# Chunk attention: the scores for the row maxima over 64 rows of the array, even and odd chunk in its two halves, issued two pairs after four exponent tiles

## Time and profile before

| | us |
|---|---|
| median of three runs | 3944.57 (3942.08 to 3945.07) |
| profiled execution, its own time | 3944.43 |
| profiled execution, span of the trace | 3942.7 |
| PE / DVE / ACT / POOL busy over the span | 3455.3 / 2757.4 / 2286.2 / 2169.0 |
| steady part of the chunk attention, 188 to 691 us: PE / DVE / ACT busy | 501.02 / 432.56 / 360.41 of 503.00 |

### The profile page before, as it was taken

The page is one execution under the profiler, slowest core; times in us unless marked ns, Lnnn a source line. Parts: engine busy times, 40 slices in busy tenths (PEclk is TensorE's granted clock), DMA queues, the critical chain, the costliest instruction groups (busy, mean ns, idle before and its releaser), DMA issues. The chain is left out here.

```text
span 3942.7 us, 89530 instructions
## 1 busy us (share of the span) xinstructions
PE 3455.3 (88%) x30494; PEld 2111.7 (54%) x30494; DVE 2757.4 (70%) x7236; ACT 2286.2 (58%) x5520; POOL 2169.0 (55%) x2263
## 2 busy tenths in 40 slices
PE   5999999985695999999999999995958885987678
PEld 1333333325592566566566566563946774775456
DVE  6888888856454778878888888873437884655565
ACT  2777777763243666666666666662436671864367
POOL 3333333315544777888887888874422332754275
PEclk7999999995697999999999999997979997987879
DMA  5434334413452222222222222222633332110001
GB/s 100 61 59 60 60 60 62 62 17 101 137 193 67 48 55 50 51 56 55 53 57 51 51 57 51 50 55 75 199 92 81 89 82 43 44 45 5 0 1 44
DMA packets 414451, 254.32 MB, mean 65 GB/s; under 512 B 251418, under 2 KB 340434, under 8 KB 412722
## 3 DMA queue, kind: packets, MB, share of 16 engines
q1 hardware_dynamic: 403316, 226.43, 25.0%
q0 software_dynamic: 10688, 22.17, 1.8%
HBM read 91.61 MB, written 45.94 MB: 35 GB/s over the span
## 5 line engine op out<-in xcount | busy, mean ns | idle before, releaser
L2799 POOL TENSOR_TENSOR ra_prob<-ra_prob,ra_inverse 128x256 f32<-128x256 f32 (+3 forms) x512 | 631.1, 1255 | 250.5 <-DVE ra_inverse L3098 249.3
L2577 DVE TENSOR_REDUCE ca_mx<-ca_ps_s 128x2 f32<-128x1024 f32 x512 | 600.6, 1211 | 120.4 <-PE ca_ps_s L2449 120.2
L3012 ACT ACTIVATE ra_prob<-ra_ps_s,ra_low 128x128 f32<-128x128 f32 (+3 forms) x1024 | 533.6, 532 | 228.5 <-DVE ra_low L3078 225.8
L2514 ACT ACTIVATE ca_pT<-ca_ps_p 128x512 f32<-128x512 f32 x1024 | 544.9, 600 | 204.6 <-PE ca_ps_p L2459 203.1
L3078 DVE CUSTOM_DVE_ANT_0 ra_ps_s<-ra_ps_s,ra_mask 128x128 f32<-128x128 f32 (+3 forms) x1024 | 479.9, 510 | 44.1 <-PE ra_ps_s L2954 43.8
L2449 PE MATMUL ca_ps_s<-ca_kst,ca_qst 128*128 128x512 bf16 x1024 | 393.0, 389 | 24.4 <-DMA ca_kst<-ca_bounce 10.9
L2459 PE MATMUL ca_ps_p<-ca_qst,ca_kst 128*128 128x512 bf16 x1024 | 386.7, 383 | 5.5 <-ACT ca_pT L2514 4.2
L3018 ACT COPY ra_probT<-ra_ps_t 128x512 f32<-128x512 f32 x384 | 227.2, 592 | 254.2 <-PE ra_ps_t L2866 254.2
L2866 PE MATMUL ra_ps_t<-ident,ra_prob 128*128 128x128 f32 x2560 | 350.1, 276 | 3.3 <-ACT ra_probT L3018 2.1
L2954 PE MATMUL ra_ps_s<-ra_kz,ra_qz 64*128 64x128 f32 (+3 forms) x2048 | 348.1, 458 | 3.8 <-DMA ra_kz<-ra_rot 2.9
L2792 POOL TENSOR_TENSOR ra_rot<-ra_prod 128x512 f32<-128x512 f32 x256 | 320.6, 1273 | 40.6 <-DVE ra_prod L3087 40.6
(11 more groups left out here) (491 smaller groups left out, 7278.5 us busy)
## 6 DMA issues: line engine op xcount, KB each, us to landing
ra_qz<-ra_rot SPq DMA_DIRECT2D x512, 64.0 KB, 2.0
ra_kz<-ra_rot SPq DMA_DIRECT2D x512, 64.0 KB, 2.0
moe_w_own<-moe_w1T SPq DMA_DIRECT2D x71, 256.0 KB
moe_w_own<-router_w SPq DMA_DIRECT2D x71, 256.0 KB
ca_kst<-ca_bounce SPq DMA_DIRECT2D x256, 64.0 KB
ca_bounce<-ca_thirds SPq DMA_DIRECT2D x192, 64.0 KB
ca_qst<-ca_bounce SPq DMA_DIRECT2D x64, 192.0 KB
moe_hs<-moe_rows SPq DMA_DIRECT2D x71, 66.0 KB, 2.1
```

Source lines behind the costliest of these rows:

```text
L2514: nc.scalar.activation(pT[:, (NS * hp + u) % PRING, :], ps_p[n % NP][:], ACT.Exp).then_inc(sg["drained"], 1)
L2577: nc.vector.tensor_reduce(mx[:, hm % 2, 2 * j:2 * j + 2], ps_s[m % 2][:].rearrange("p (b k) -> p b k", b=2), AX.X, ALU.max)\
L2799: nc.gpsimd.tensor_tensor(at, at, inverse[:, n % PROB, 2 * tile:2 * tile + 2].unsqueeze(2).broadcast_to([P, 2, keys]), ALU.mult)\
L3012: nc.scalar.activation(prob[:, n % PROB, tile, head, 0:keys], part(n, tile)[:, head, :], ACT.Exp, bias=low[:, n % PROB, at:at + 1], scale= ...
```

```diff
-                        sp.dma_start(qst[ROWS:ROWS + 2, s, :], zeros).then_inc(qk_ready[s], 16)
                         for lo, hi in Q_ROWS:
                             sp.dma_start(qst[lo:hi, s, :]...)
                         for r, (_, tk) in enumerate(THIRDS):
                             sp.dma_start(kst[r * DK:(r + 1) * DK, s, :]...)
+                        wait(sp, sg["s_in"], PAIRS * (hf - 1))
+                        odd = bounce[s].rearrange("o (a two) x d g t -> two o (x d) a (g t)", two=2)[1]
+                        for lo, hi in Q_ROWS:
+                            sp.dma_start(qodd[ROWS + lo:ROWS + hi, hf % 2, :]..., odd[0, 0:hi - lo]).then_inc(odd_ready[hf % 2], 16)
+                        for r, (_, tk) in enumerate(THIRDS):
+                            sp.dma_start(kodd[ROWS + r * DK:ROWS + (r + 1) * DK, hf % 2, :]..., odd[1, tk * DK:(tk + 1) * DK])\
+                                .then_inc(odd_ready[hf % 2], 16)
...
-                def score(k, h):
-                    a, qt = k // 4, k % 4
-                    if k == 0:
+                def scores(j, h):
+                    a, qt = j // 4, j % 4
+                    if j == 0:
                         pe.wait_ge(qk_ready[h % RING], times(h, RING, COPIES))
-                    m = s_use[h, k // 2]
-                    out = pair(m) if k % 2 == 0 else ps_s[m % 2]
-                    ins = nc.tensor.matmul(out[:, k % 2 * 512:(k % 2 + 1) * 512], chunk(qst, P, h, a, qt), chunk(kst, P, h, a), start=True, stop=True)
-                    if k % 2:
-                        ins.then_inc(sg["s_in"], 1)
+                        pe.wait_ge(odd_ready[h % 2], times(h, 2, COPIES))
+                    out = pair(s_use[h, j])
+                    nc.tensor.matmul(out[:, 0:512], chunk(qst, ROWS, h, 2 * a, qt), chunk(kst, ROWS, h, 2 * a), start=True, stop=True)
+                    nc.tensor.matmul(out[:, 512:1024], qodd[ROWS:2 * ROWS, h % 2, a * 512 + qt * P:a * 512 + (qt + 1) * P],
+                                     kodd[ROWS:2 * ROWS, h % 2, a * 512:(a + 1) * 512], start=True, stop=True).then_inc(sg["s_in"], 1)
...
-                        if hm is not None:
-                            score(u, hm)
+                        if hm is not None and u % 4 == 3:
+                            for j in (u // 2 - 1, u // 2):
+                                scores(j, hm)
```

More of the change, by code:

```diff
@@ L2233, in chunk_attention @@
     Q_ROWS = ((0, 24), (24, 48), (48, 64))
-    COPIES = len(Q_ROWS) + len(THIRDS) + 1
+    COPIES = len(Q_ROWS) + len(THIRDS)
     RING = 4
-    VRING = 6
+    VRING, VW = 6, 16
     PRING = 12
@@ L2257, in chunk_attention @@
     sbounce = nc.dram_tensor(f"{name}_sbounce", (2, 2, NS, P), BF16, kind="Internal").ap()
-    zeros = nc.dram_tensor(f"{name}_zeros", (2, CG * HT), BF16, kind="Internal").ap()
     with ExitStack() as ctx:
@@ L2272, in chunk_attention @@
         kst = sb("kst", [P, RING, CG * HT], BF16)
-        vst = sb("vst", [P, VRING, NC, 4, 32])
+        qodd, kodd = sb("qodd", [P, 2, CG * HT // 2], BF16), sb("kodd", [P, 2, CG * HT // 2], BF16)
+        vst = sb("vst", [P, VRING, NC * 4 + 1, VW])
         mx = sb("mx", [P, 2, NS])
@@ L2284, in chunk_attention @@
         ps_p = [pb(f"ps_p{i}") for i in range(NP)]
-        loaded, prep, zeroed = sem("loaded"), sem("prep"), sem("zeroed")
+        loaded, prep = sem("loaded"), sem("prep")
         q_set, k_set, v_set = sem("q_set"), sem("k_set"), sem("v_set")
@@ L2294, in chunk_attention @@
         qk_ready = [sem(f"qk_ready{i}") for i in range(RING)]
+        odd_ready = [sem(f"odd_ready{i}") for i in range(2)]
         sbounced = [sem(f"sbounced{i}") for i in range(2)]
@@ L2307, in _ @@
                 sp.wait_ge(q_set, 1)
-                sp.dma_start(zeros, qst[ROWS:ROWS + 2, 0, :]).then_inc(zeroed, 16)
-                sp.wait_ge(zeroed, 16)
                 sp.wait_ge(k_set, 1)
@@ L2323, in body @@
                             sp.dma_start(kst[r * DK:(r + 1) * DK, s, :].rearrange("p (a c) -> p a c", a=NC), rows[1, tk * DK:(tk + 1) * DK]).then_inc(qk_ready[s], 16)
+                        wait(sp, sg["s_in"], PAIRS * (hf - 1))
+                        odd = bounce[s].rearrange("o (a two) x d g t -> two o (x d) a (g t)", two=2)[1]
+                        for lo, hi in Q_ROWS:
+                            sp.dma_start(qodd[ROWS + lo:ROWS + hi, hf % 2, :].rearrange("p (a c) -> p a c", a=NC // 2), odd[0, 0:hi - lo]).then_inc(odd_ready[hf % 2], 16)
+                        for r, (_, tk) in enumerate(THIRDS):
+                            sp.dma_start(kodd[ROWS + r * DK:ROWS + (r + 1) * DK, hf % 2, :].rearrange("p (a c) -> p a c", a=NC // 2), odd[1, tk * DK:(tk + 1) * DK])\
+                                .then_inc(odd_ready[hf % 2], 16)
                     if ht is not None:
@@ L2468, in values @@
                         a = 4 * g + b
-                        last = nc.tensor.matmul(ps_o[b * 32:(b + 1) * 32, :], vst[:, h % VRING, a, kt, :], pT[:, (NS * h + 4 * r + b) % PRING, :],
+                        last = nc.tensor.matmul(ps_o[b * 32:(b + 1) * 32, :], vst[:, h % VRING].rearrange("p n d -> p (n d)")[:, (4 * a + kt) * VW:(4 * a + kt) * VW + 32], pT[:, (NS * h + 4 * r + b) % PRING, :],
                                                 start=(kt == 0), stop=(kt == 3))
@@ L2505, in front_part @@
                             act.wait_ge(sg["pv_done"], 8 * (h - VRING + 1))
-                        nc.scalar.copy(vst[:, h % VRING, :, :, 0:DK], ps_p[n % NP][:, 0:HT].rearrange("p (a k d) -> p a k d", a=NC, k=4)).then_inc(sg["drained"], 1)
+                        nc.scalar.copy(vst[:, h % VRING, 0:NC * 4, 0:DK], ps_p[n % NP][:, 0:HT].rearrange("p (n d) -> p n d", d=DK)).then_inc(sg["drained"], 1)
                 def body(h, ht, hp):
@@ L2522, in _ @@
                 for ring in range(0, VRING, 3):
-                    at = vst[:, ring:ring + 3].rearrange("p r a k d -> p (r a k) d")
-                    blank = core.ones[:, 0:1].unsqueeze(2).broadcast_to([P, 3 * NC * 4, 32])
+                    at = vst[:, ring:ring + 3].rearrange("p r n d -> p (r n) d")
+                    blank = core.ones[:, 0:1].unsqueeze(2).broadcast_to([P, 3 * (NC * 4 + 1), VW])
                     nc.scalar.activation(at, blank, ACT.Copy, scale=0.0).then_inc(v_set, 1)
@@ L2527, in _ @@
                 for ring in range(0, VRING, 3):
-                    at = vst[:, ring:ring + 3, :, :, DK].rearrange("p r a k -> p (r a k)")
-                    nc.scalar.copy(at, core.ones[:, 0:1].broadcast_to([P, 3 * NC * 4])).then_inc(v_set, 1)
+                    at = vst[:, ring:ring + 3, :, DK].rearrange("p r n -> p (r n)")
+                    nc.scalar.copy(at, core.ones[:, 0:1].broadcast_to([P, 3 * (NC * 4 + 1)])).then_inc(v_set, 1)
                 static_steps(NHALF, (FRONT, TURN, PROB), body)
@@ L2576, in body @@
                             m = s_use[hm, j]
-                            nc.vector.tensor_reduce(mx[:, hm % 2, 2 * j:2 * j + 2], ps_s[m % 2][:].rearrange("p (b k) -> p b k", b=2), AX.X, ALU.max)\
+                            nc.vector.tensor_reduce(mx[:, hm % 2, :].rearrange("p (a x q) -> p a x q", x=2, q=4)[:, j // 4, :, j % 4], ps_s[m % 2][:].rearrange("p (b k) -> p b k", b=2), AX.X, ALU.max)\
                                 .then_inc(sg["max_done"], 1)
@@ L2582, in chunk_attention @@
         mv, sq, tot, msq = sb("mv", [P, NB, 2]), sb("sq", [P, NB, 2]), sb("tot", [P, NB, 2]), sb("msq", [P, NB])
-        rs, half, yn = sb("rs", [P, NB]), sb("half", [P, NB]), sb("yn", [P, 2, 4 * D])
+        rs, half, yn = sb("rs", [P, NB]), sb("half", [P, NB]), pT[:, 0:2, :]
         dv, pw, nd, ad, nd2 = sem("dv"), sem("pw"), sem("nd"), sem("ad"), sem("nd2")
```

## The result

The changed kernel takes 3987.28 us (median of four runs, 3981.59 to 3996.76), the kernel before 3944.82 us beside it: a ratio of 1.0117, 95% interval 1.0104 to 1.0131. Slower by 1.2%, and the forecast of 3987 us lies on it. The profiled execution took 3982.44 us, 38.0 us more than that of before.

The account below looks back on a forecast made before the run. PE was taken to bound the steady part at 25.18 us a step. To 3944.4 us it added 28 for 30 steps 0.93 us longer, 7 for maxima waits and 8 at the start: 3987 us, range 3955 to 4028.

Parts of the forecast that it names:

- PE sets the pace of the steady part: Steady chunk attention: PE busy 501.02 of 503.00 us, 25.18 us a step; DVE next at 21.6 us a step.
- A pair costs one matmul: Scores on TensorE: two 64-row matmuls run side by side, saving 3.45 us a step.
- A third change of mode, 0.09 us: Each group on TensorE gets one more change of mode: 0.09 us, 0.74 us a step.
- The fourth tile waits 0.42 us: With three banks, each group's fourth exponent tile waits 0.42 us for ScalarE, starting 1.08 us after the first.
- Groups with other products, +0.1, so 0.93 us a step on PE: Groups with transposes, V or Q and K add net 0.1 us to the plain groups' 0.8 us a step.
- VectorE, net 0: Input norm delays one pair about 0.5 us a step, offset by half of the old kernel's 1.2 us hiccups.
- Waits for the maxima, +7 us, and +8 at the start: Eleven odd loads on SyncE delay the maxima: about 0.3 us a step, plus 4.2 us twice at the start.
- Sum: Whole kernel: 3944.4 + 28 + 7 + 8 = 3987.5 us, predicted as 3987 us.
- the halves pay: Rival: the fourth tile does not wait, group 2.51 us, step about 22.7 us, time 3872 us; chance 6%.
- The transfers bind: Rival: odd loads take 5.5 us or more, each step waits 1.5 to 2.5 us, 4025 to 4055 us; 14%.
- No overlap: Rival: a pair's bf16 matmuls don't overlap, or mode changes cost far more: +104 us, 4090 us; 3%.
- Signs: New profile: group near 2.93 us, fourth tile released by ACT, pair starts within 0.01 us, step near 26.1 us, DVE 83%.

Follow-up runs that it names:

- VectorE out of the way: Each maximum taken over the first 256 of 512 keys, in the changed kernel and in the kernel before: 3964.17 and 3929.68 us.
- e1_order_only: Kernel before with only the order changed: four exponent tiles, then four scores, all over 128 rows; 4028.89 us.
- e6_after_maxima_first: Changed kernel with the maxima's write ahead of the even loads on SyncE's queue, read-back between even and odd loads; 3990.02 us, ratio 1.0099.

## Why the prediction was right, point by point

- *PE sets the pace of the steady part*: right. What lengthened PE's list of waits lengthened the step.
- *A pair costs one matmul*: right, 0.23 us from pair to pair.
- *A third change of mode, 0.09 us*: 0.104 us. Right within a hundredth or two.
- *The fourth tile waits 0.42 us*: right, 1.08 us from first to fourth tile in the changed kernel and with the order alone. The row at the stage's end in the old trace was the changed group in advance.
- *Groups with other products, +0.1, so 0.93 us a step on PE*: 0.96 with VectorE out of the way. Right, and in its parts too: between these two runs the group with the transposes grows by 0.32 us (3.10 to 3.42) and the last group not at all (4.49 and 4.48); forecast 0.35 and nothing.
- *VectorE, net 0*: mis-sized. It is +0.24 us a step (0.64 against 0.40), 7 us in 30 steps. The prediction set a wait of 0.5 us behind the input norm against 0.6 us that it took from the kernel before. The wait is 0.45 us; but what falls away is only 0.40, and the values' waits for the transposes, 0.18 us a step, were not in the sum.
- *Waits for the maxima, +7 us, and +8 at the start*: mis-sized. In this execution 3.9 us at the start of step 4 and some 1.6 us in later steps. The first scores come at 44.57 us, 3.2 us late (forecast 4.2, at 45.6); the forecast then added another 4.2 for step 4's first tile, but only 0.8 us came on top. The prediction let the odd loads push everything by their own time; but the maxima's write, issued 3.8 us later in the step, landed sooner after its issue (median 5.9 us where it was 7.2), and the longer step left room. Why it landed sooner is not shown. Only in shorter steps, with the loads alone or a pair after every two tiles, do they show as 12 and 17 us of waits.
- *Sum*: the stage became 41.75 us longer, forecast 43 (3944.4 and 43 is 3987.4, where it wrote 3987.5). Steps gave 8 us more and the transfers 9 less than forecast. These two misses cancel; the mechanism was right, the hit to the microsecond is luck, the more so as single runs of the changed kernel scatter over 15 us.
- *Rivals*: "the halves pay" needed a group whose fourth tile does not wait. Such an order exists: with a pair after every two tiles, and its transfers out of the way, it is 0.3% faster than the kernel before. "The transfers bind" is ruled out by the runs without most loads and with the maxima first. "No overlap", or a far dearer change of mode, is ruled out by the starts of a pair, 0.01 us apart or less, and by 0.104 us a change.
- *Signs*: the group, the fourth tile, its releaser and the pairs' starts came as listed, and three first tiles were released by the transfer of the maxima. The step is 26.37 us where 26.1 was listed, VectorE's share of the steady part 410.11 / 503 = 82% where it was 83.

## What to carry to other kernels

Before shortening work on the engine that sets the pace, ask what that work covers. Here the scores stood between exponent tiles and covered ScalarE's emptying of a ring of three banks; halving them is worth something only as long as the first and the (ring + 1)-th tile stay as far apart as fill, read and release take (1.08 us here). Here a step lost 3.16 us by the order, 0.83 by changes of mode and 0.64 by VectorE, against 3.45 saved. The end of a pipeline, where one kind of work has run out, often shows in the old trace what a step looks like without it. And when a step gets shorter, look again at transfers that had room to spare: the same loads cost about 5 us beside a 26.4 us step and 17 beside a 25.2 us one.

## What was not expected of the hardware

The maxima's small write lands after 1.4 us ahead of the bulk loads and after 6 to 7 us behind them (medians; at most 9.8), on one queue. With eleven more loads ahead of it, it landed sooner after its own issue in the changed kernel, not later (median 5.9 against 7.2); why stays open. The rest of the program, whose instructions no run touched, took from about 3030 us (`e1_order_only`) to about 3049 us (`e6_after_maxima_first`) from the stage's end to the span's; what makes it differ stays open.
